# A decoder layer on one core: the attention steps planned by halves, with more of the cross attention inside them

## What is computed

```python
# x: (16, 128, 256) f32; 16 batches of 128 tokens; ctx_1024 the same shape
x = x + diff_attention(layernorm(x))      # 16 heads, 2 x 8 wide, softmax(q1 k1) v - lam * softmax(q2 k2) v,
                                          # each head's 16 outputs divided by their root mean square, W_proj
x = x + gelu(cross(layernorm(x), ctx, ctx) @ Wf.T + bf) + ctx     # one head, 256 wide, temperature 8
x = x + swiglu_shared(layernorm(x)) + sum_over_top_2_of_16(gate_e * swiglu_e(layernorm(x)))
```

## Time and profile before

| | |
|---|---|
| three executions | 633.18, 634.68, 641.69 us; median 634.68 |
| the profiled execution | 638.05 us, span 636.8 us, mean granted TensorE clock 0.938 |
| busy in the span | TensorE 556.8 us (87%), VectorE 312.4, ScalarE 227.4, GpSimd 221.4 |
| chain that ended last | TensorE 37%, issue 20%, VectorE 14%, DMA 12%, GpSimd 11%, ScalarE 5% |

### The profile page before, as it was taken

The page is one execution under the profiler, slowest core; times in us unless marked ns, Lnnn a source line. Parts: engine busy times, 40 slices in busy tenths (PEclk is TensorE's granted clock), DMA queues, the critical chain, the costliest instruction groups (busy, mean ns, idle before and its releaser), DMA issues.

```text
span 636.8 us, 9896 instructions
## 1 busy us (share of the span) xinstructions
PE 556.8 (87%) x3274; PEld 335.3 (53%) x3274; DVE 312.4 (49%) x677; ACT 227.4 (36%) x422; POOL 221.4 (35%) x449
## 2 busy tenths in 40 slices
PE   4933988869989979599999989996999999999998
PEld 2522435336555546465567538455556666665447
DVE  5634877884698754756334454210222322222282
ACT  6311564643735535446341410110333333333110
POOL 2421465755725434221101004654233334333100
PEclk9975897969989979899789999999899999999999
DMA  7697549536532419800006935222123332331631
GB/s 203 202 190 118 99 103 217 107 68 185 103 62 48 135 56 158 247 1 1 1 0 198 348 114 178 87 76 84 57 84 90 89 89 83 89 90 64 238 122 62
DMA packets 62192, 72.39 MB, mean 114 GB/s; under 512 B 14816, under 2 KB 55264, under 8 KB 60608
## 3 DMA queue, kind: packets, MB, share of 16 engines
q1 hardware_dynamic: 58352, 61.37, 38.9%
q0 software_dynamic: 3792, 10.39, 4.7%
HBM read 45.31 MB, written 26.03 MB: 112 GB/s over the span
## 4 chain that ended last, share of the span: by engine, by line
PE 37%; issue 20%; DVE 14%; DMA 12%; POOL 11%; ACT 5%; SPq 1%; POOLq 0%; DVEq 0%; ACTq 0%
PE ps L516 9%; DMA x_slots<-XN,slot_i 7%; POOL y_rows L1445 7%; PE ps L527 5%; PE ps L378 4%; PE ps L320 3%; PE ps L366 2%; ACT prob L1183 2%; DVE nmax L795 2%; PE ps L347 2%; PE ps L440 2%; PE ps L461 2%; PE ps L449 2%; PE ps L334 1%; DMA pack_k<-qk_parts 1%
## 5 line engine op out<-in xcount | busy, mean ns | idle before, releaser
L795 DVE TENSOR_REDUCE nmax<-ps 128x8 f32<-128x1024 f32 x64 | 77.8, 1216 | 51.2 <-PE ps L347 51.0
L571 PE MATMUL ps<-W,xt 128*128 x188 | 91.0, 607 | 0.6 <-ACT xt L1273 0.3
L1445 POOL DMA_INDIRECT y_rows<-yo,goes_to x47 | 45.8, 975 | 91.9 <-DVE yo L1002 91.9
L1183 ACT ACTIVATE prob<-ps 128x1024 f32<-128x1024 f32 x64 | 65.4, 1023 | 33.5 <-PE ps L366 33.5
L995 DVE TENSOR_TENSOR sa<-sa,ps 128x256 f32<-128x256 f32 x47 | 19.8, 421 | 99.9 <-ACT sa L1280 99.9
L516 PE MATMUL ps<-xT,W1s 128*128 128x512 f32 x128 | 62.6, 612 | 0.8 <-DVE yo L1002 0.8
L516 PE MATMUL ps<-xT,W2s 128*128 128x512 f32 x128 | 61.5, 603 | 0.0
L527 PE MATMUL ps<-W3s,hTs 128*128 128x256 f32 x256 | 58.2, 389 | 2.6 <-DVE hTs L928 2.6
L928 DVE TENSOR_TENSOR hTs<-sil,ps 128x512 f32<-128x512 f32 x32 | 22.0, 688 | 69.3 <-PE ps L516 57.5
L527 PEld LDWEIGHTS ps<-W3s,hTs 128*128 128x128 f32 x256 | 49.6, 195 | 11.9 <-DVE hTs L928 5.1
L1266 ACT ACTIVATE sil<-ps 128x512 f32<-128x512 f32 x32 | 19.1, 597 | 100.0 <-PE ps L516 99.9
(11 more groups left out here) (182 smaller groups left out, 865.7 us busy)
## 6 DMA issues: line engine op xcount, KB each, us to landing
W<-in_L_ffn_routed_w_dram SPq DMA_DIRECT2D x12, 1024.0 KB, 11.8
qk_parts<-part SPq DMA_DIRECT2D x28, 256.0 KB, 4.3
pack_q<-qk_parts SPq DMA_DIRECT2D x48, 128.0 KB, 3.8
pack_k<-qk_parts SPq DMA_DIRECT2D x48, 128.0 KB, 4.4
xg<-x_slots SPq DMA_DIRECT2D x47, 129.0 KB, 2.1
x_slots<-zero SPq DMA_DIRECT2D x11, 512.0 KB, 11.1
yg<-y_rows SPq DMA_DIRECT2D x4, 1024.0 KB, 8.6
X<-in_x_dram SPq DMA_DIRECT2D x4, 512.0 KB, 8.1
```

What stands on the lines that cost most here:

```text
L571: r = t.matmul(ps[:, 2 + p, :], xt[:, p, k, :], W12[:, ds(e, 1), k, :].rearrange("p o f -> p (o f)"), start=(k == 0), stop=(k == KT - 1))
L795: v.tensor_reduce(nmax[:, s % 4, a, :, :], ps[:, 0:2, :].rearrange("p m (h t) -> p m h t", h=4), AX_X, ALU.max, negate=True).then_inc(maxe ...
L1183: a.activation(prob[:, n:n + 2, :], ps[:, 2:4, :], ACT.Exp, scale=HD ** -0.5).then_inc(exped, 1)
L1445: g.indirect_dma_start(out=y_rows, out_offset=bass.IndirectOffsetOnAxis(ap=goes_to[:, n:n + 1].bitcast(U32), axis=0), in_=yo[:, p, :], in_ ...
```

## The change

- `PROJECTED = 3`: chunks 0, 1 and 2 are normalized, turned and projected (`qk`) before the steps, chunk 2 with a second `xT_2`; chunk 2's `values` stay in the steps.
- 36 transposes of the identity run on TensorE at the start, and VectorE copies half of `Wqk` before it normalizes chunk 0.
- The first six `scores` alternate between banks 0, 1 and 2, 3; `exps(0, 0)` waits for all six maxima.
- Each piece on DVE, ACT and TensorE has a place (s, a) in a table. VectorE's `between` runs in each half, before the second `max_of` and after it. The root is in two parts, scaling and transpose are apart. GpSimd's bias and context additions are per batch. `pv(s, 0)` stands before `turn_max`.
- The context and keys of chunk 3, and of chunks 0 and 1 `turn`, `cross_scores`, `max_cross`, `exp_cross`, `turn_p`, `weigh_values` and `put_fo`, are in the steps (`INSIDE = 2`); `gelu` and `add_cross` of these stay behind them. `fo` has two buffers.
- `fetch` writes its 16 rows three partitions apart. The stores of chunk 1 and 2 are issued in steps 0 and 4, and fetch(1) in two halves around `put_max(0)`.
- The cross stage is written out anew for chunks 2 and 3, and begins with `norm3` of chunk 0.

```diff
-Q_RUNS = [(0, 1), (2, 1), (4, 0)]
-K_RUNS = [(0, 0), (2, 1), (4, 2)]
+
+Q_RUNS = [1, 1, 0]
+K_RUNS = [0, 1, 2]
...
+WARM = 36
...
-TURN_AT = {2: 1, 3: 9}
-VALUES_AT = {2: 8, 3: 16}
-CTX_AT = {0: 17, 1: 22, 2: 27}
-OUT_AT = {0: 20, 1: 25, 2: 30}
-WEIGHTS_AT = 14
-LIFT_AT = 7
+PROJECTED = 3
+TURN_AT = (4, 0)
+QK_AT = ((5, 0), (6, 0), (7, 0), (8, 0))
+VALUES_AT = {2: ((8, 1), (9, 0)), 3: ((17, 0), (17, 1))}
+LIFT_AT = (7, 0)
+WF_AT, A_AT, B_AT, M_AT = (9, 1), (10, 0), (10, 1), (11, 0)
+CTX_AT = {0: (11, 1), 1: (15, 1), 2: (18, 0), 3: (24, 1)}
+KEYS_AT = {0: ((12, 0), (12, 1)), 1: ((16, 0), (16, 1)), 2: ((19, 1), (20, 0)), 3: ((25, 0), (25, 1))}
+KEYS_IN = {0: (6, 7), 1: (6, 7), 2: (7, 7), 3: (6, 7)}
+U_AT = {0: ((14, 1), (15, 0)), 1: ((22, 0), (22, 1)), 2: ((29, 1), (30, 0))}
+OUT_AT = {0: ((13, 0), (13, 1)), 1: ((23, 0), (23, 1)), 2: ((30, 1), (31, 0))}
+
+CLIP_AT = {0: 8, 1: 16, 2: 24}
+SQUARE_AT = {0: (9, 1), 1: (17, 1), 2: (25, 1)}
+SUM_AT = {0: (10, 0), 1: (18, 0), 2: (26, 0)}
+ROOT_AT = {0: ((10, 1), (11, 0)), 1: ((18, 1), (19, 0)), 2: ((26, 1), (27, 1))}
+NORM_AT = {0: (11, 1), 1: (20, 0), 2: (28, 0)}
+OT_AT = {0: (12, 0), 1: (20, 1), 2: (28, 1)}
+ADD_AT = {0: (14, 0), 1: (24, 0), 2: (31, 1)}
+STATS_AT = {0: (14, 1), 1: (24, 1)}
+SCALE_AT = {0: 15, 1: 25}
+NORMAL_AT = {0: (16, 1), 1: (25, 1)}
+ROWS_AT = {0: (18, 1), 1: (26, 0)}
+SCORES_AT = {0: (19, 0), 1: (26, 1)}
+MAX_AT = {0: (19, 1), 1: (27, 0)}
+EXP_AT = {0: (20, 0), 1: (27, 1)}
+TURN_P_AT = {0: (20, 1), 1: (28, 0)}
+WEIGH_AT = {0: (21, 0), 1: (28, 1)}
+FO_AT = {0: (21, 1), 1: (29, 0)}
+CONTEXT_AT = {0: 18, 1: 27}
+INSIDE = 2
...
+        def scores_bank(n):
+            return n % 2 * 2 if n < 2 * LEAD else 0
...
+                if n >= 2 * LEAD:
                     t.wait_ge(maxed, n)
+                elif n >= 2:
+                    t.wait_ge(maxed, n - 1)
...
+                    t.wait_ge(maxed, 2 * LEAD)
...
-            for c in range(2):
+            for _ in range(WARM):
+                t.transpose(ps[:, 0, 0:P], ident[:, :], ident[:, :])
+            for c in range(PROJECTED):
                 turn(norm, c, 4, xn)
                 if c == 0:
                     t.wait_ge(wqk_put, 1)
                     t.wait_ge(Wv_loaded, 16)
                 for f in range(4):
                     qk(c, f)
-                for i in range(2):
-                    values(c, i)
-
-
-            t.wait_ge(rests, 8)
+                if c < 2:
+                    for i in range(2):
+                        values(c, i)
+
+
+            t.wait_ge(rests, 4 * PROJECTED)
...
+            t.wait_ge(router_in, 32)
+            t.wait_ge(shared_in, 48)
+            turn(norm3, 0, 4, rows(XN, 0))
+            up(0, 0)
+            t.wait_ge(norm3.put, 2)
+            turn(norm, NC + 2, 4, xn)
+            cross_scores(2)
+            route_logits(0)
+            up(0, 1)
+            up(0, 2)
+            turn_p(2)
+            for i in range(2):
+                project_values(NC - 1, i, 2 + i)
+            for i in range(2):
+                project_o(NC - 1, i, 4 + i)
+            up(0, 3)
+            weigh_values(2)
+            t.wait_ge(x_added, 2 * NC)
+            turn(norm3, 1, 4, rows(XN, 1))
+            up(0, 4)
+            t.wait_ge(norm3.put, 4)
+            turn(norm, NC + 3, 4, xn)
+            t.wait_ge(fo_put, CB * 3)
+            up(0, 5)
+            cross_scores(3)
+            route_logits(1)
+            up(0, 6)
+            turn_p(3)
+            up(0, 7)
+            t.wait_ge(logits_put, 2)
+            turn(norm3, 2, 4, rows(XN, 2))
+            t.wait_ge(u_put, 2 * NC)
+            down(0, 0)
+            weigh_values(3)
+            route_logits(2)
+            for j in range(1, CB):
+                down(0, j)
+            up(1, 0)
...
+            def root_o(part_):
+                if part_ == 0:
+                    start_root(yo_[:, :], va[:, :])
+                    improve_root(yo_[:, :], va[:, :])
+                else:
+                    improve_root(yo_[:, :], va[:, :])
+                    improve_root(yo_[:, :], va[:, :])
+                    step(v.tensor_tensor(yo_[:, :], yo_[:, :], fits[:, :], ALU.mult))
...
+
             for j in range(LEAD):
                 for a in range(2):
                     max_of(j, a)
+            prepare_weights()
             for s in range(STEPS):
                 if s + LEAD < STEPS:
                     max_of(s + LEAD, 0)
                 if s:
                     turn_o(s - 1)
                     invert(s - 1)
+                else:
+                    make_lambda()
+                between(s, 0)
                 if s + LEAD < STEPS:
                     max_of(s + LEAD, 1)
+                between(s, 1)
             turn_o(STEPS - 1)
             invert(STEPS - 1)
 
 
+            v.wait_ge(x_added, 2 * (NC - 1))
+            stats(norm, NC + 2, 2)
+            add_cross(0)
+            v.wait_ge(x_done, 2)
+            stats(norm3, 0, 0)
+            v.wait_ge(combined, STEPS)
+            sum_o(NC - 1)
+            normalize(norm3, 0, 0, rows(XN, 0))
+            normalize(norm, NC + 2, 2, xn)
+            root_o(0)
+            gate_up(0, 0)
+            root_o(1)
+            norm_o(NC - 1)
+            turn_attn(NC - 1)
+            max_cross(2)
+            add_cross(1)
+            put_logits(0)
+            v.wait_ge(x_done, 4)
+            stats(norm3, 1, 1)
+            gate_up(0, 1)
+            gate_up(0, 2)
+            normalize(norm3, 1, 1, rows(XN, 1))
+            add_o(NC - 1, 4)
+            v.wait_ge(x_added, 2 * NC)
+            stats(norm, NC + 3, 3)
+            gate_up(0, 3)
+            normalize(norm, NC + 3, 3, xn)
+            put_fo(2)
+            gate_up(0, 4)
+            add_cross(2)
+            v.wait_ge(x_done, 6)
+            stats(norm3, 2, 2)
+            gate_up(0, 5)
+            max_cross(3)
+            put_logits(1)
+            normalize(norm3, 2, 2, rows(XN, 2))
+            gate_up(0, 6)
+            gate_up(0, 7)
+            add_shared(0, 0)
+            put_fo(3)
+            put_logits(2)
+            add_shared(0, 1)
+            add_cross(3)
+            v.wait_ge(x_done, 8)
+            stats(norm3, 3, 3)
             add_shared(0, 2)
...
+            gelu(0)
+            gelu(1)
+            put_turned(norm3, 0, 4, xT3[0])
+            silu_up(0, 0)
+            put_turned(norm, NC + 2, 4, xT, 1.0)
+            silu_up(0, 1)
+            exp_cross(2)
+            put_p(2)
+            silu_up(0, 2)
+            for i in range(2):
+                put_u(NC - 1, i, 2 + i)
+            silu_up(0, 3)
+            put_turned(norm3, 1, 4, xT3[1])
+            gelu(2)
+            silu_up(0, 4)
+            put_turned(norm, NC + 3, 4, xT, 1.0)
+            silu_up(0, 5)
+            exp_cross(3)
+            silu_up(0, 6)
+            put_p(3)
+            silu_up(0, 7)
+            put_turned(norm3, 2, 4, xT3[2])
+            gelu(3)
...
-                for n, (tile, f, (r0, p0)) in enumerate(
-                        [(Qp[u], half, run) for run in Q_RUNS] + [(Kp[u], 2 + half, run) for run in K_RUNS]):
+                q.wait_ge(parts_stored[c], 16 * STORES)
+                runs = [(Qp[u], half, run) for run in enumerate(Q_RUNS)] + [(Kp[u], 2 + half, run) for run in enumerate(K_RUNS)]
+                for n, (tile, f, (r0, p0)) in enumerate(runs):
                     if n in pieces:
                         for m in range(2):
-                            to = MG * m + r0 * HD
-                            q.dma_start(tile[to:to + 2 * HD, :, :].rearrange("p h t -> p (h t)"),
+                            q.dma_start(tile[MG * m + r0:MG * m + KQ:3, :, :].rearrange("p h t -> p (h t)"),
                                         qk_parts[c, f, p0:p0 + 2, :, m * HU:(m + 1) * HU, :].rearrange(
                                             "q d h t -> (q d) (h t)")).then_inc(packed[u], 16)
...
             fetch(0, range(PIECES))
-            for i in range(3):
-                store_part(1, i)
-            fetch(1, range(PIECES))
             for s in range(LEAD - 1):
+                fetch(1, range(3 * s, 3 * s + 3))
                 put_max(s)
             for s in range(STEPS):
                 if s + LEAD - 1 < STEPS:
                     put_max(s + LEAD - 1)
-                for c, s0 in TURN_AT.items():
-                    if s == s0 + 5:
-                        store_part(c, 0)
-                    if s == s0 + 6:
-                        store_part(c, 1)
-                        store_part(c, 2)
-                if s // CB + UNITS - 1 < STEPS // CB and s % CB < 3:
-                    fetch(s // CB + UNITS - 1, range(2 * (s % CB), 2 * (s % CB) + 2))
+                if s in (0, CB):
+                    for i in range(3):
+                        store_part(1 + s // CB, i)
+                if s == QK_AT[3][0] + 1:
+                    store_part(3, 0)
+                if s == QK_AT[3][0] + 2:
+                    store_part(3, 1)
```

(5 more changed lines are left out.)

533 lines of the change are left out of this document (230 added, 303 removed).

## The result

| | before | after |
|---|---|---|
| median of the executions | 633.93 us (631.72 to 641.69) | 624.99 us (623.42 to 629.11) |
| ratio | | 0.986, 95% interval 0.981 to 0.990 |
| profiled execution, span | 638.05, 636.8 us | 624.47, 623.2 us |
| mean granted clock | 0.938 | 0.945 |

A forecast was written before the change was run, and what follows sets the result against it. TensorE was taken to bound the attention steps and cross stage, leaving idle and low-clock time to save. Prologue -8.4, steps -2 and cross stage -16 sum to -26.4: 634.7 becomes 608 us, range 597 to 622.

The forecast's parts named there:

- I carried the difference: Whole kernel: profiled execution 638.05 us lay 3.4 over the 634.68 median; the saving was subtracted from 634.7.
- Part 1, the prologue: Start to first exponential: warm projections, spread fetch rows and alternating banks bring it to 52.9 from 61.3, -8.4 us.
- Part 2, the steps: Attention steps, first to last exponential: pieces moved in and out, shared among halves, 182 us against 183.9, -2 us.
- The price of the steps: Attention steps: TensorE's pieces plus 1.48 us per half with a piece and 1.65 per empty half; 168.4 us.
- the warm 130.1: Steps 9 to 31 at the prediction's prices for pieces and halves, TensorE at its higher clock: 130.1 us.
- the 12 that I took: Attention steps: loss over the price where VectorE exceeds TensorE's own time, 12 us, bounds 4 and 20.
- Two more sources: Attention steps: put_max(1) and half of fetch(2) queued on SP behind bulk issues, at most 1.5 us once.
- list of steps in which VectorE is over: Steps 7, 14, 18, 24, 26, 27, 28: VectorE over TensorE's own time by 0.5 to 3 us, 12 in sum.
- the 1.65 us for an empty half: Half a step without a TensorE piece: one matmul group and one exponential in the same banks decide, 1.65 us.
- the warm price: Steps at the higher clock: 1.48 us per half with a piece, 1.65 without, plus the pieces.
- Part 3, the cross stage: Last exponential to `up(1,0)`: work moved into the steps, new 8 us idle at the start; 85 for 101.6, -16 us.
- VectorE as the bound: Attention steps: VectorE becomes the bound, loss 20 to 22 us, cross stage's start idles 3 longer; 620 us, chance 0.20.

The follow-up runs named there:

- c1: The changed kernel, unaltered, timed again beside the follow-up kernels; 625.72 us, ratio 0.980 to the kernel before.
- e9: Changed kernel with chunk 1's stores before the first maxima, chunk 2's in step 2, fetch(2) in steps 0 and 1, `lift_queries` in step 2; 614.29 us, ratio 0.960.
- e7: Changed kernel with chunk 1's stores issued before the first maxima and chunk 2's in step 0; 618.63 us, ratio 0.970 to the kernel before.
- e1: Changed kernel with chunk 2's stores issued in step 1 instead of step 4; 624.64 us, ratio 0.978 to the kernel before.
- e2: Changed kernel with fetches to 16 neighbouring partitions instead of every third of 48; 629.05 us, ratio 0.985 to the kernel before.

## Why the prediction missed

**The sum against one execution.** 12.8 us of the 16.7 missed lie between the two profiled executions (638.05 to 624.47, -13.6 against -26.4). The other 3.9 come from the base: the profiled execution of before was 3.4 us over the median of 634.68 that the forecast used (4.1 over the 633.93 of four executions), and that of after 0.5 under its own. "I carried the difference" took as an offset what was the scatter of one execution.

**Part 1, the prologue, was right in after:** -8.8 for -8.4. In c1 it was -7.3, since the start was cold there, so that the last 1.6 us depend on the execution. First `scores` at 44.16 (forecast 43.9), released by the projection and not by the fetch, first exponential at 52.4 (52.9), 2.8 us for the warm projections (2.6), maxima 1.15 apart (1.27). The rule of the Trainium skill that stood beside the prediction, "SBUF — State Buffer", "Door 1: The DMA port swizzle", gives about 109 GB/s for four ports and about 218 for eight; that the spread rows reach eight, and so the 218, is an estimate worked out from its formula. The stretches show 129 and 201 GB/s: the direction is right, but the gain is 1.6 times and not twice, and neighbouring rows are faster than the Trainium skill has them.

**Part 2, the steps, is where it failed:** +15.7 for -2. The price of the steps was about right from step 9 on: steps 9 to 31 cost 8.3 us over the warm 130.1, less than the 12 that I took, and the longest wait of `scores` on `nmax` in steps 24 to 31, 1.20 us, was within the forecast. The failed step is the sentence "Two more sources: put_max(1) and half of fetch(2) are queued on SP behind bulk issues, at most 1.5 us once". It followed the maxima and the fetch, and left out who waits for the *stores* that the change moves behind them: `put_first(3,0)` with the exponentials of ScalarE behind it, and `combine(0)` with `split_max` behind it on GpSimd. Where it put 1.5 us, steps 5 to 8 lose 12.9, together with `lift_queries` in step 7 (35.1 in after, 22.2 in e9). e7, which touches the stores alone, gives back 8.1 of it, and e9's move of `lift_queries` 4.4. Step 7 was on the prediction's list of steps in which VectorE is over, so a part of these 4.4 stood in its 12 us. The second fault is in the 1.65 us for an empty half. It came from step 6 of before, where the clock was 1.00 and the DMA share 0.20 (90.9:94.3). In 55:80 of after they are 0.67 and 0.51, and steps 0 to 4 cost 8.8 us over the price; how much of it is the clock and how much the queue stays an estimate, as said above. Of the 31.2 us over the warm price, 14.1 are thus in steps 5 to 8, 8.8 in steps 0 to 4 and 8.3 behind.

**Part 3, the cross stage, was right and too careful:** 82.2 us for 85, with the idle start of 8.8 (forecast 8) and the cold `up(0,0)` as described.

**The rivals.** The one nearest in time, VectorE as the bound (620 us), has the wrong cause: over the 199.6 us of the steps VectorE is busy 142, and in steps 5 to 8 TensorE's two longest waits are for ScalarE (3.78 us) and for the DMA (2.46); the one for VectorE behind `lift_queries` is 1.66. None of the rivals held a wait on stores. With these waits and `lift_queries` taken out, e9 stands at 0.960 of the kernel before, and the forecast was 608.3 / 634.7 = 0.958. That the two agree is luck in part: e9 takes 614.3 us and not 608, its steps take 189.0 us where 182 was forecast, the cross stage is 3 us better than forecast, and the kernel before was 2.7 us slower in that session than the 634.7.

## What to carry to other kernels

When a bulk transfer is moved later in a queue, list all that waits for its end: not only who reads the data, but who overwrites its source or a buffer that shares its place, and what stands behind that instruction on its engine. Several late things can hide behind one another: here undoing one showed nothing (e1) where undoing more of them did (e7 to e9). Take the price of a step from a stretch whose queue and clock are those of the stretch that is forecast, and weigh the profiled execution against the median before a difference is carried.

## What was not expected of the hardware

The spread rows cost SP more to issue. Timelines of SP, six pieces of fetch(0) in after and in e2:

```profile
30.17 3.77 SPq L1661 DMA_DIRECT2D pack_q<-qk_parts  x6
```

```profile
30.72 2.65 SPq L1661 DMA_DIRECT2D pack_q<-qk_parts  x6
```

0.63 us for a piece against 0.44. At 128 KB a piece that is 208 GB/s, about the 201 measured, so with spread rows one engine issues the fetch hardly faster than it runs. In 32:36 of after the DMA engines had room beside it (share 0.70), from 36 to 42 little (0.96), at the same rate. Whether a second issuing engine would make the fetch faster is therefore open. Two stretches of after, columns as in the earlier trace rows:

```profile
32.00:36.00 4.00, 3.21 (x19) 2.60 (x18) 3.26 (x11) 2.17 (x4) 2.82 (x4) 1.00 0.70 197
36.00:42.00 6.00, 6.00 (x15) 2.66 (x14) 2.54 (x5) 1.79 (x3) 2.71 (x3) 1.00 0.96 201
```

With plain rows (e2) the engines are busy throughout at 125 GB/s:

```profile
36.00:46.00 10.00, 7.34 (x32) 3.14 (x30) 4.76 (x9) 2.39 (x4) 5.59 (x6) 1.00 1.01 125
```
